# One wait less ahead of the second expert's gathers in a mixture-of-experts kernel

## The chip, the cores and the metric

The kernel runs on one core of one Trainium2 chip. The metric is the device time of one execution in microseconds (us); less is better. The core has five engines, each with its own instruction stream: PE (TensorE, matmuls), DVE (VectorE), ACT (ScalarE), POOL (GpSimd) and SP (SyncE, which here only issues DMAs). They meet at semaphores: an instruction may wait until a semaphore has reached a number, and everything behind it on that engine waits too.

## The reference, cut to what matters

One block of a network on x of 4 x 1024 tokens with 256 features each:

```
x = x + 0.5 * ffn(layernorm(x))
x = x + attention(layernorm(x))        # 16 heads, causal
x = x + 0.5 * ffn(layernorm(x))

# ffn: 8 experts, top 2, capacity C = 1280 tokens for each expert
logits = xf @ Wg ; probs = softmax(logits) ; top_vals, top_idx = top_k(probs, 2)
buf    = tokens put into (expert, place), dropped where place >= C
a, g   = split(buf[e] @ W_in[e])       # 256 -> 2 x 512
out_e  = (gelu(a) * g) @ W_out[e]      # 512 -> 256
y      = sum over the two choices of gate * out_e, back at the token's row
```

Both ffn calls use the same weights, so the kernel runs the same mixture twice, with the attention between them.

## The kernel before, in words

A mixture has two functions. `route` normalizes the tokens, writes them to a table in DRAM (`normalized`, rows of 264 floats: 256 features and the gates), and makes for each expert the list of its 1280 tokens (`token`, 10 tiles of 128 places). It signals `list_ready` = 1 when the first expert's list stands, 2 when those of the seven others do, and 3 when the rows for the way back (`sum_row`) do.

`experts` then goes through the 8 experts, e = 0 to 7, in the same order on each engine:

- POOL brings the expert's rows into SBUF: 10 gathers (indirect DMAs through `gather_slots`, L254), each for 128 rows of 1056 bytes. There are two buffers, `slots[0]` for the even experts and `slots[1]` for the odd ones. Once results are ready it sends them: 10 indirect DMAs (L908) that add 128 result rows each onto the table `sums`. The code has expert e+1's gathers ahead of expert e's sends. The first expert's own gathers are issued by `route` (6) and at the head of `experts` (4).
- PE turns the gathered rows (`transposes`, L1107, in three chunks; each sends one `s_tposed`), multiplies them by W_in (`up`, L1128), and the gated hidden values by W_out (`down`, L1147). float32 values are split into a high and a low part, so each product takes three matmuls. For the first expert the chunks hold 256, 512 and 512 tokens, for the others 512, 512 and 256.
- ACT takes the high part of the turned rows (`s_hi`, L1037), applies the GELU (L1051), takes the high part of the next expert's weights (`w_hi`, L1070) and scales the results (`res`, L1063).
- DVE takes the low parts (`s_lo` L948, `w_lo` L999), multiplies GELU and gate half (`hid`, L968) and splits the product (L971 high, L973 low). PE's `up` has two PSUM buffers: block f may start once DVE's `hid` of block f-2 is done.
- SP loads the next expert's W_in and W_out (1.5 MB, L263 and L265) into the single buffer `raw`, once DVE has done the low parts of the present ones.

The order on each engine is written out by hand. In POOL's loop a gather into `slots` stands behind the condition that the rows that the buffer held have been turned: before expert e+1's gathers POOL waits for `s_tposed` to reach 3 e, which is the count after expert e-1's three chunks. For e = 0, whose gathers fill `slots[1]` for the first time in the mixture, it waits for `list_ready` = 2 and for `s_tposed` = 3, the first expert's three chunks, which are read from `slots[0]`.

Of the kernel before, what the change touches and what calls it, by code (L numbers as in the profile page):

```python
# [250 lines left out]
def gather_slots(pool, held, xn_dram, e, j):  # L251

    at = e * ST + j
    pool.indirect_dma_start(held["slots"][e % 2][:, j * ROW:(j + 1) * ROW], None, xn_dram,  # L254
                            bass.IndirectOffsetOnAxis(ap=held["token"][:, at:at + 1], axis=0)).then_inc(slots_sem(held, e, j), 16)
# [584 lines left out]
def experts(kit, c, r, w_in_dram, w_out_dram, xn_dram, sum_dram, held, out_dram):  # L840
# [4 lines left out]
    with ExitStack() as ctx:  # L845
# [23 lines left out]
        NC, NW = len(CHUNKS), len(W_PARTS)  # L869
# [29 lines left out]
        def gpsimd(pool):  # L899
            last_row = nc.gpsimd.to_reg(TOK + CAP - 1)  # L900

            def send(e, ci):
                c0, n = CHUNKS[ci]
                for j in range(c0 // P, (c0 + n) // P):
                    pool.wait_ge(res_ready, e * ST + j + 1 + RES0)
                    kit.part(pool)
                    at = e * ST + j
                    nc.gpsimd.indirect_dma_start(sum_dram, bass.IndirectOffsetOnAxis(ap=sum_row[:, at:at + 1], axis=0), res[j][:], None,  # L908
                                                 bounds_check=last_row, oob_is_err=True, compute_op=ALU.add).then_inc(added, 16)

            for j in range(EARLY_TILES, ST):
                gather_slots(nc.gpsimd, held, xn_dram, 0, j)
            for e in range(EXP):
                if e + 1 < EXP:
                    if e == 0:
                        pool.wait_ge(list_ready, 2)
                        pool.wait_ge(s_tposed, NC)
                    if e:
                        pool.wait_ge(s_tposed, e * NC)
                    for j in range(ST):  # L920
                        gather_slots(nc.gpsimd, held, xn_dram, e + 1, j)
                if e:
                    pool.wait_ge(added, e * ST * 16)
                else:
                    pool.wait_ge(c["zeroed"], 2 * 16)
                    pool.wait_ge(held["sums_out"], 16)
                    pool.wait_ge(list_ready, 3)
                pool.sem_inc(res_free, 1)
                for ci in range(NC):
                    send(e, ci)  # L930
            pool.wait_ge(added, EXP * ST * 16)
# [164 lines left out]
        def tensor(pe):  # L1096
# [72 lines left out]
            in_turn(nc.tensor, body)  # L1169

        return {"sync": sync, "gpsimd": gpsimd, "vector": vector, "scalar": scalar, "tensor": tensor}

# [1108 lines left out]
```

## Time and profile before

| | |
|---|---|
| three executions, us | 1628.95, 1629.88, 1635.23; median 1629.88 |
| the profiled execution: its own time, its span in the trace, us | 1629.88, 1627.9 |
| PE busy | 1442.2 us (89% of the span) |
| DVE busy | 1022.1 us (63%) |
| ACT busy | 711.3 us (44%) |
| POOL busy | 703.3 us (43%) |
| the 160 gathers on POOL (L254), us | 167.8 busy, mean 1.049 |
| the 160 sends on POOL (L908), us | 271.4 busy, mean 1.696 |
| clock granted to TensorE, mean | 0.941 of full speed |

The first mixture's experts fill about 62 to 430 us of the span and the second's about 1239 to 1610. A gather's or a send's time on POOL is that of making its descriptors; the transfer runs behind it on 16 DMA engines, which all queues share.

### The profile page before, as it was taken

Reading aid. Unit: us, or ns where it says so; the run is one execution under the profiler, and the core shown is the slowest. Engines: PE = TensorE matmul, PEld = TensorE weight load, DVE = VectorE, ACT = ScalarE, POOL = GpSimd, SP = SyncE. Lnnn points to the kernel's source line nnn. Section 1 sums busy time; section 2 is a strip of 40 time slices with the busy share of each in tenths; the row PEclk is TensorE's granted clock in tenths of the full one; section 3 lists DMA queues with packets and bytes.
Section 4 is the critical chain, followed back from the end, with each engine's and each line's share of the span. In section 5 each row is a group of like instructions: output and inputs, shape, how many; then the busy total and the mean of one; then the engine's idle time right before and its main releaser. Section 6 shows DMA issues by size and latency. Waiting matters only on the chain. (4 is left out here: it accounts for less than half of the span.)

```text
span 1627.9 us, 25426 instructions
## 1 busy us (share of the span) xinstructions
PE 1442.2 (89%) x8838; PEld 1085.9 (67%) x8840; DVE 1022.1 (63%) x2599; ACT 711.3 (44%) x1116; POOL 703.3 (43%) x653
## 2 busy tenths in 40 slices
PE   4699999999545799999999999999877999999994
PEld 3588888889544455555555555555556888888884
DVE  7755665555275777777777777886376555665551
ACT  5333333333223055656656565666553333333331
POOL 1375556564423433333333332224303755556533
PEclk9799999999867689999999999999887999999997
DMA  9554444452377936666667568553173544444426
GB/s 313 144 109 96 98 96 65 95 105 33 54 212 210 251 112 165 175 164 163 166 160 183 146 180 246 169 167 92 42 245 81 115 93 96 96 99 64 95 33 136
DMA packets 125559, 218.26 MB, mean 134 GB/s; under 512 B 20232, under 2 KB 86280, under 8 KB 122312
## 3 DMA queue, kind: packets, MB, share of 16 engines
q1 hardware_dynamic: 88824, 165.56, 35.4%
q0 software_dynamic: 30720, 42.62, 16.6%
q10 hardware_dynamic: 5904, 8.66, 1.8%
q8 instruction: 62, 1.02, 0.3%
q14 instruction: 49, 0.40, 0.1%
HBM read 130.56 MB, written 90.14 MB: 136 GB/s over the span
## 5 line engine op out<-in xcount | busy, mean ns | idle before, releaser
L2025 ACT ACTIVATE a_wts<-a_s_psum 128x1024 f32<-128x1024 f32 (+1 forms) x384 | 300.8, 809 | 181.6 <-PE a_s_psum L2142 179.5
L908 POOL DMA_INDIRECT sums<-e_res,e_sum_row x160 | 271.4, 1696 | 245.6 <-ACT e_res L1063 215.7
L1901 DVE CUSTOM_DVE_ANT_0 a_m_psum<-a_m_psum,mask 128x128 f32<-128x128 f32 (+3 forms) x512 | 249.1, 502 | 128.5 <-PE a_m_psum L2117 120.8
L2117 PE MATMUL a_m_psum<-a_kp,a_qp 96*128 96x512 f32 (+2 forms) x768 | 288.6, 410 | 25.2 <-DVE a_parts L1901 9.8
L2117 PEld LDWEIGHTS a_m_psum<-a_kp,a_qp 96*128 96x128 f32 x768 | 148.8, 196 | 144.8 <-DVE a_parts L1901 61.4
L1051 ACT ACTIVATE e_act_a<-e_a_psum 128x512 f32<-128x512 f32 (+1 forms) x192 | 100.4, 527 | 278.2 <-PE e_a_psum L1128 254.0
L1849 POOL TENSOR_SCALAR_AFFINE_SELECT a_wts<-a_wts 128x512 f32<-128x512 f32 x128 | 78.2, 634 | 332.4 <-ACT a_wts L2025 332.4
L968 DVE TENSOR_TENSOR e_hid<-e_act_a,e_g_psum 128x512 f32<-128x512 f32 (+1 forms) x192 | 114.5, 596 | 157.3 <-PE e_g_psum L1128 139.9
L2142 PE MATMUL a_s_psum<-a_qp,a_kp 97*128 97x512 f32 (+2 forms) x768 | 210.0, 356 | 0.4 <-ACT a_wts L2025 0.2
L254 POOL DMA_INDIRECT e_slots<-normalized,e_token x160 | 167.8, 1049 | 92.5 <-issue 46.9
L1147 PE MATMUL e_o_psum<-e_w_hi,e_h_hi 128*128 128x256 f32 x640 | 183.5, 287 | 0.0
L1904 DVE TENSOR_REDUCE a_parts<-a_m_psum 128x1 f32<-128x512 f32 x256 | 176.4, 689 | 9.1 <-PE a_m_psum L2117 6.6
L1147 PE MATMUL e_o_psum<-e_w_hi,e_h_lo 128*128 128x256 f32 x640 | 181.2, 283 | 0.0
L1147 PE MATMUL e_o_psum<-e_w_lo,e_h_hi 128*128 128x256 f32 x640 | 181.2, 283 | 0.0
L2156 PE MATMUL a_o_psum<-a_wts,a_vg 128*17 128x512 f32 (+3 forms) x1536 | 157.2, 497 | 4.2 <-POOL a_wts L1849 2.7
L1128 PE MATMUL e_a_psum<-e_s_hi,e_w_hi 128*128 128x512 f32 (+1 forms) x384 | 141.9, 370 | 18.5 <-DVE e_hid L968 10.0
L2142 PEld LDWEIGHTS a_s_psum<-a_qp,a_kp 97*128 97x128 f32 x768 | 133.5, 191 | 19.0 <-ACT a_wts L2025 4.9
L1063 ACT ACTIVATE e_res<-e_o_psum,e_gate 128x256 f32<-128x256 f32 x160 | 76.0, 475 | 148.7 <-PE e_o_psum L1147 147.7
L1128 PE MATMUL e_a_psum<-e_s_lo,e_w_hi 128*128 128x512 f32 (+1 forms) x384 | 137.3, 358 | 0.0
L1128 PE MATMUL e_a_psum<-e_s_hi,e_w_lo 128*128 128x512 f32 (+1 forms) x384 | 137.1, 357 | 0.0
L1128 PE MATMUL e_g_psum<-e_s_hi,e_w_hi 128*128 128x512 f32 (+1 forms) x384 | 137.0, 357 | 0.0
L1128 PE MATMUL e_g_psum<-e_s_hi,e_w_lo 128*128 128x512 f32 (+1 forms) x384 | 136.8, 356 | 0.0
(270 smaller groups left out, 2560.6 us busy)
## 6 DMA issues: line engine op xcount, KB each, us to landing
packs<-x_res SPq DMA_DIRECT2D x48, 512.0 KB, 5.8
e_w_raw<-in_W_in SPq DMA_DIRECT2D x16, 1024.0 KB, 8.2
a_qp<-packs SPq DMA_DIRECT2D x16, 1024.0 KB, 7.8
a_kp<-packs SPq DMA_DIRECT2D x16, 1024.0 KB, 13.7
e_w_raw<-in_W_out SPq DMA_DIRECT2D x16, 512.0 KB, 8.3
normalized<-r_xn SPq DMA_DIRECT2D x16, 512.0 KB, 4.4
sums<-x_res SPq DMA_DIRECT2D x2, 4096.0 KB, 16.5
x_res<-sums SPq DMA_DIRECT2D x8, 1024.0 KB, 11.3
```

The source lines that it names most:

```text
L254: pool.indirect_dma_start(held["slots"][e % 2][:, j * ROW:(j + 1) * ROW], None, xn_dram, bass.IndirectOffsetOnAxis(ap=held["token"][:, at: ...
L908: nc.gpsimd.indirect_dma_start(sum_dram, bass.IndirectOffsetOnAxis(ap=sum_row[:, at:at + 1], axis=0), res[j][:], None, bounds_check=last_r ...
L968: nc.vector.tensor_tensor(hid[q][:, 0:n], act_a[q][:, 0:n], g_ps[q][:, 0:n], ALU.mult).then_inc(hid_done, 1)
L1051: nc.scalar.activation(act_a[q][:, 0:n], a_ps[q][:, 0:n], ACT.Gelu).then_inc(gelu_done, 1)
L1128: last = nc.tensor.matmul(bank[q][:, 0:n], w_in_at(w, k, half + f), s[:, k, c0:c0 + n], start=(z == 0), stop=(z == len(terms) - 1))
L1147: last = nc.tensor.matmul(o_ps[(u * ST + c0 // P + j) % 2][:, 0:D], s[:, k, j * P:(j + 1) * P], w_out_at(w, k), start=(z == 0), stop=(z == ...
L1901: nc.vector.tensor_tensor_reduce(products, products, c["mask"][:, QC - width:], 1.0, MASKED, ALU.add, ALU.max, top).then_inc(max_read, 1)
L1904: nc.vector.reduce_max(top, products, AX.X).then_inc(max_read, 1)
L2025: nc.scalar.activation(wts[(u * NS + s) % 2][:, j, 0:w], s_ps[q % 2][:, 0:w], ACT.Exp).then_inc(weighed, 1)
L2117: nc.tensor.matmul(m_ps[bank((n, h, z))][:, 0:stream], qp[n % NB][0:PACK, h, qt * P:(qt + 1) * P], kp[n % NB][0:PACK, h, part * QC:part * ...
L2142: last = nc.tensor.matmul(s_ps[q % 2][:, col - lead:col + w], kp[u][:, j, kt * P:(kt + 1) * P], qp[u][:, j, at - lead:at + w], start=True, ...
L2156: last = nc.tensor.matmul(o_ps[j * HP:j * HP + HV, q0:q0 + w], vg[u][:, kt, j, :], wts[(u * NS + s) % 2][:, j, col:col + w], start=(kt == ...
```

## The change

In `experts`, in POOL's stream, the wait for `s_tposed` = 3 ahead of the second expert's gathers is taken out. It stood once in each mixture, so the program loses two waits. The wait for `list_ready` = 2 stays, and so do the waits of all later experts.

```diff
                 if e + 1 < EXP:
                     if e == 0:
                         pool.wait_ge(list_ready, 2)
-                        pool.wait_ge(s_tposed, NC)
                     if e:
                         pool.wait_ge(s_tposed, e * NC)
                     for j in range(ST):
```

On POOL, at the head of the first mixture's experts, the rows are the following (a piece of the difference; `e_slots` are the buffers, `normalized` the table of rows, `x9` nine equal instructions, `experts_s_tposed` the semaphore of the wait):

```order
 L254 DMA e_slots<-normalized,e_token 128x264 [waits route_list_ready,route_gates_out,route_rows_out]
 L254 DMA e_slots<-normalized,e_token 128x264 x9
-L254 DMA e_slots<-normalized,e_token 128x264 [waits experts_s_tposed,route_list_ready]
+L254 DMA e_slots<-normalized,e_token 128x264 [waits route_list_ready]
 L254 DMA e_slots<-normalized,e_token 128x264 x9
 L908 DMA sums<-e_res,e_sum_row 5376x256 [waits route_list_ready,const_zeroed,route_sums_out,experts_res_ready]
```

No instruction has another place. The first of the second expert's ten gathers has one condition less; the ten sends of the first expert stand behind them as before. The other engines' streams are the same but for line numbers.

## Rows read from the trace of the kernel before

**Rows 1.** Timeline of POOL, first mixture: start us, us, instruction, [idle before <-releaser]

```profile
68.56 0.95 POOL L254 DMA_INDIRECT e_slots<-normalized,e_token  x1 [0.30 <-issue]
82.23 1.46 POOL L254 DMA_INDIRECT e_slots<-normalized,e_token  x1 [12.73 <-PE e_tp_psum L1107]
...
95.55 0.94 POOL L254 DMA_INDIRECT e_slots<-normalized,e_token  x1 [0.30 <-issue]
96.79 1.63 POOL L908 DMA_INDIRECT sums<-e_res,e_sum_row  x1 [0.30 <-issue]
...
104.32 1.56 POOL L908 DMA_INDIRECT sums<-e_res,e_sum_row  x1 [4.01 <-ACT e_res L1063]
...
117.34 1.55 POOL L908 DMA_INDIRECT sums<-e_res,e_sum_row  x1 [0.30 <-issue]
```

**Rows 2.** Timeline of POOL, second mixture

```profile
1241.42 1.59 POOL L254 DMA_INDIRECT e_slots<-normalized,e_token  x1 [0.30 <-issue]
1257.98 1.47 POOL L254 DMA_INDIRECT e_slots<-normalized,e_token  x1 [14.97 <-PE e_tp_psum L1107]
```

**Rows 3.** Waits of PE, 67 to 118 us: engine, line, releaser: total us, times, longest

```profile
PE e_a_psum L1128 <- DVE e_hid L968: 0.2, 1, 0.2
```

**Rows 4.** Timeline of PE, first mixture, and a row of the second

```profile
74.86 0.47 PE L1128 MATMUL e_a_psum<-e_s_hi,e_w_hi 128*128 128x512 f32 x1 [0.20 <-DVE e_hid L968]
...
81.23 0.48 PE L1128 MATMUL e_a_psum<-e_s_hi,e_w_hi 128*128 128x512 f32 x1
...
84.05 0.39 PE L1128 MATMUL e_a_psum<-e_s_hi,e_w_hi 128*128 128x512 f32 x1
...
100.55 1.03 PE L1107 MATMUL e_tp_psum<-ident,e_slots 128*128 128x128 f32 x8
...
1256.98 0.47 PE L1128 MATMUL e_a_psum<-e_s_hi,e_w_hi 128*128 128x512 f32 x1
```

**Rows 5.** Stretches: A:B, us, PE, PEld, DVE, ACT, POOL busy (count), PEclk, DMA share, GB/s

```profile
60.00:64.00 4.00, 2.10 (x29) 1.71 (x26) 1.08 (x3) 1.14 (x1) 3.06 (x4) 1.00 0.40 109
...
70.00:72.00 2.00, 2.00 (x20) 2.00 (x19) 1.00 (x3) 0.56 (x2) 0.00 (x0) 1.00 1.09 415
72.00:74.00 2.00, 2.00 (x19) 2.00 (x18) 1.93 (x5) 1.15 (x3) 0.00 (x0) 1.00 0.97 311
74.00:76.00 2.00, 1.80 (x11) 1.44 (x10) 1.90 (x6) 1.25 (x2) 0.00 (x0) 1.00 0.17 55
```

**Rows 6.** Timeline of ACT, first and then second mixture

```profile
73.98 0.38 ACT L1051 ACTIVATE e_act_a<-e_a_psum 128x256 f32<-128x256 f32 x1 [0.85 <-PE e_a_psum L1128]
75.12 1.05 ACT L1070 CAST e_w_hi<-e_w_raw 128x1024 fp32r<-128x1024 f32 x1 [0.75 <-DMA e_w_raw<-in_W_out]
76.53 0.60 ACT L1051 ACTIVATE e_act_a<-e_a_psum 128x512 f32<-128x512 f32 x1 [0.36 <-PE e_a_psum L1128]
...
88.48 0.47 ACT L1063 ACTIVATE e_res<-e_o_psum,e_gate 128x256 f32<-128x256 f32 x1 [1.35 <-PE e_o_psum L1147]
...
1250.31 1.04 ACT L1070 CAST e_w_hi<-e_w_raw 128x1024 fp32r<-128x1024 f32 x1
1252.29 0.60 ACT L1051 ACTIVATE e_act_a<-e_a_psum 128x512 f32<-128x512 f32 x1 [0.94 <-PE e_a_psum L1128]
```

**Rows 7.** A stretch of the second mixture, same columns

```profile
1248.00:1250.00 2.00, 2.00 (x19) 2.00 (x18) 1.07 (x1) 1.18 (x2) 0.00 (x0) 1.00 0.43 150
```

**Rows 8.** Timeline of DVE, first and then second mixture

```profile
78.08 0.69 DVE L968 TENSOR_TENSOR e_hid<-e_act_a,e_g_psum 128x512 f32<-128x512 f32 x1 [1.46 <-PE e_g_psum L1128]
...
81.00 0.68 DVE L968 TENSOR_TENSOR e_hid<-e_act_a,e_g_psum 128x512 f32<-128x512 f32 x1
...
1253.83 0.69 DVE L968 TENSOR_TENSOR e_hid<-e_act_a,e_g_psum 128x512 f32<-128x512 f32 x1 [1.44 <-PE e_g_psum L1128]
```

**Rows 9.** One of DVE's groups, 82 to 98 us: busy us, mean ns | idle

```profile
L971 DVE CAST e_h_hi<-e_hid 128x512 fp32r<-128x512 f32 x5 | 2.4, 474 | 0.2
```

**Rows 10.** The same group, 98 to 119 us

```profile
L971 DVE CAST e_h_hi<-e_hid 128x512 fp32r<-128x512 f32 x3 | 1.3, 426 | 0.1
```

## The prediction

> **What bounds the kernel now.** I read the timeline of POOL first, since the change stands there. After its last gather for the first expert (start 68.56 us) POOL sits idle for 12.73 us until PE's third chunk of transposes, then issues the second expert's ten gathers from 82.23 to 96.49 (95.55 + 0.94), and goes straight on to the sends [rows 1]. The second mixture has the same picture, with 14.97 us of idle time [rows 2]. The change opens these two gaps. Idle time of an engine is worth something only if another one waits for it, so the next view is that of PE's waits: from 67 to 118 us, which covers the gap, the gathers and the sends, PE waits once, 0.2 us, for DVE [rows 3]. It never waits for a gather. PE turns the second expert's rows at 100.55 [rows 4], 4.1 us after POOL is done with the gathers, and runs into that instruction with no idle time. So in this stretch the kernel goes at PE's pace, and neither POOL nor the gathered rows set it. What earlier gathers could still do is disturb somebody, so the last views are the DMA share by stretch, ACT's and DVE's timelines and DVE's durations beside gathers.
>
> **The start of the gathers.** The one wait left is for the lists of the seven other experts. POOL's queue has the first expert's gathers ahead of it, the last of them ending at 68.56 + 0.95 = 69.5, and the lists must stand by then, since PE is busy without a gap with the first expert's products from 70 on [rows 5], and its part in the lists comes ahead of them in its stream. With the 0.30 us between two gathers the second expert's begin at about 69.8 in place of 82.2, 12.4 us earlier, and end at about 84.1. In the second mixture they begin at 1241.42 + 1.59 + 0.30 = 1243.3 in place of 1258.0, 14.7 us earlier. Worth to PE: 0, because the rows were there in time already.
>
> **The sends behind them.** The first result is ready at 88.48 + 0.47 = 88.95 [rows 6], but its send starts at 96.79, behind the gathers [rows 1]. It will start at about 89.0, 7.8 us earlier, and the second soon after. The third waits for ACT again, 4.01 us, and starts at 104.32, and from there the sends run one behind the other to the last at 117.34. ACT's results come from PE, so the third and the last stay where they are. The lead of the first two is lost again within the expert; the gathers for the third expert, which follow the last send, don't move. Worth 0.
>
> **The weights of the second expert.** This is the one transfer that the moved gathers run into. SP loads 1.5 MB for ACT, and ACT waits for it already: it is free at 73.98 + 0.38 = 74.36 and starts the high part at 75.12, released by that DMA [rows 6]. The DMA engines are full from 70 to 74 (shares 1.09 and 0.97) and at 0.17 from 74 to 76, so the load ends at about 74.3 [rows 5]. Gathers alone, at POOL's pace, take 0.40 of the engines and move 109 GB/s (60 to 64 us, same rows). The first moved gather's descriptors are out at about 70.8. From then 3.5 us of full engines are left of the load; with 0.6 of the engines that is 3.5 / 0.6 = 5.8 us, a delay of 2.3 us. If both get halves it is 7.0 us, a delay of 3.5.
>
> How much of a delay does PE not see? The high part would end at 76.17, the GELU behind it starts at 76.53 because PE is not ready before: 0.36 us. That GELU ends at 77.13, and DVE's product starts at 78.08, held by PE [rows 8]: 0.95 us. The product ends at 78.77 and frees the PSUM buffer that PE takes at 81.23: 2.46 us. Together 3.8. The next product, 81.00 to 81.68, has 2.37 us to PE's 84.05, with DVE busy in between: 0.36 + 0.95 + 2.37 = 3.7. So delays of 2.3 and 3.5 both cost nothing, the latter barely; the cover is gone from 3.7 on, and then each microsecond counts.
>
> In the second mixture ACT does not wait for the load: it starts at 1250.31 [rows 6], and the share of 0.43 from 1248 to 1250 says that the load ends at about 1248.9 [rows 7]. From 1244.3, when the moved gathers begin to transfer, 4.6 us are left; over 0.6 that is 7.7 us, to 1252.0, 1.7 us after ACT's start (with halves 9.2 us, 3.2 after). The slack is 0.94 up to the GELU at 1252.29, 0.94 up to the product at 1253.83 [rows 8], and from its end, 1254.5, to PE at 1256.98 [rows 4] 2.46: together 4.3. Again 0.
>
> **DVE beside POOL's gathers.** While ten gathers ran (82 to 98 us) DVE's copy of 512 columns took 474 ns as a mean of five [rows 9]; from 98 to 119, beside sends, it took 426 [rows 10]. That is 0.05 us each, 0.24 for the five. This disturbance moves to 70 to 84 us. From 70.9 to 76.6 DVE goes without a pause and PE waits for it (the 0.2 us at 74.86 [rows 4]), so there a share of it reaches PE; further on DVE's products have 2.4 us to PE's need. About half of the gathers fall into the tight part: 0.12 us a mixture, 0.2 for both. The bounds are +0.5 (all ten, both mixtures) and -0.4 (PE's wait of 0.2 gone in both; I have no mechanism for more, since PE has no other idle time to give back). I take +0.2, near the measured copies.
>
> The Trainium skill has a rule that speaks against this change: in "SBUF — State Buffer", section "SBUF: two separate sides", the port pair of DVE and GpSimd is an exclusive lock, and the loser is blocked for the whole instruction. By it a copy that meets a gather would wait up to the gather's full time. The trace bears out at most a small part of that, with 48 ns more on the mean copy; it is the second rival below.
>
> **Sum.** The profiled execution took 1629.88 us (span 1627.9, 2.0 around it), which is also the median of the three runs. Gathers 0, sends 0, weights 0, DVE +0.2: 1630.1 us. Changes below 0.5% (8.1 us) are what a measurement of this kernel can't tell from none; one run of three was itself 5.3 above the median.
>
> **Rivals.**
>
> *The weights come too late (slower).* Place: ACT's high part of the second expert's weights, both mixtures. It decides from a delay of 3.7 us in the first and 4.3 in the second. If the load got nothing until all ten gathers were issued, it would end at 84.1 + 3.5 = 87.6, a delay of 13.3, and PE would lose 9.6; in the second mixture, with 14.3 us for ten gathers as in the first, 1243.3 + 14.3 + 4.6 = 1262.2 against 1250.3, 11.9, and a loss of 7.6. Together 17.2, that is 1647.1 at the far end. I price it at half: 1638.5. For it: ACT already waits 0.75 us for that DMA and the engines are full just then. Against: the gathers come at POOL's pace and leave 0.6 of the engines. 4%.
>
> *DVE is held by the gathers (slower).* Seven copies of DVE (four of 256 columns, three of 512) fall between 70 and 82 us (PE's blocks there, one copy each; an estimate from its pace). Were each held for a whole gather of 0.95, DVE would be 6.7 us late, less 2.4 of slack: 4.3 a mixture, 8.6 in all, 1638.5. Against it are rows 9. 3%.
>
> *The first two sends count (faster).* If the first expert's end hung on its sends, 7.8 us would be gained in each mixture: 1614.3. For it: the first result waits 7.8 us for POOL. Against: POOL waits for ACT before the third send, and PE waits for nothing. 2%.
>
> *Nothing moves.* The gathers start no earlier because another condition holds POOL (the lists, or room for descriptors in its queue): 1629.9. The 12.73 us are put down to PE's transposes, which speaks against. 3%.
>
> **How the numbers follow.** 88% for the forecast, 1630.1. Its own spread is the scatter of the runs rather than the terms: 1628.0 to 1634.5 holds it 8 or 9 times in 10 and leaves out the two slower rivals and the faster one, together 9%. Slower by over 0.5%: the two slower rivals at their price and above, with what an unlucky set of runs adds, 5%. Faster by over 0.5%: 3%. Within: 92%.
>
> **What the next profile would show.** Right: POOL's idle time before the second expert's gathers gone, their starts near 69.8 and 1243.3; the first send near 89, the third still near 104.3 with its wait for ACT; PE's transposes of the second expert still near 100.5; ACT's first high part of the second expert later by 1 to 3 us, with a longer wait for the DMA, and PE's blocks at 81.2 and 84.0 unmoved. Wrong: PE waiting several microseconds for DVE or ACT between 78 and 90 us (the weights), DVE's copies near 1 us (the lock), or PE's transposes of the second expert more than a microsecond away from 100.5.

## The result, and the profile after

| | before | after |
|---|---|---|
| executions, us | 1628.95 to 1635.23, median 1630.58 (4) | 1649.62 to 1659.21, median 1657.14 (4) |
| ratio, 95% interval | | 1.0156 (1.0134 to 1.018) |
| profiled execution, its span, us | 1629.88, 1627.9 | 1641.82, 1640.0 |
| granted TensorE clock, mean | 0.941 | 0.934 |

Beside the profiled one and these four, ten more executions of the changed kernel are on record, 1654.98 to 1664.46 us. The ratios here and in the experiments are the record's estimates, each with its interval, and not quotients of the two medians (that would be 1.0163 here).

The changed kernel is 1.56% slower. The prediction was 1630.1 us, 1628.0 to 1634.5: no change. POOL's timeline of the changed kernel, first mixture (start, us, instruction, [idle before <-releaser]):

```profile
68.35 0.94 POOL L254 DMA_INDIRECT e_slots<-normalized,e_token  x1 [0.30 <-issue]
69.60 0.95 POOL L254 DMA_INDIRECT e_slots<-normalized,e_token  x1 [0.30 <-issue]
...
80.89 0.95 POOL L254 DMA_INDIRECT e_slots<-normalized,e_token  x1 [0.30 <-issue]
103.96 1.73 POOL L908 DMA_INDIRECT sums<-e_res,e_sum_row  x1 [22.12 <-ACT e_res L1062]
...
118.46 1.57 POOL L908 DMA_INDIRECT sums<-e_res,e_sum_row  x1 [10.33 <-ACT e_res L1062]
...
131.48 1.55 POOL L908 DMA_INDIRECT sums<-e_res,e_sum_row  x1 [0.30 <-issue]
```

The gathers did what was foreseen: the second expert's begin at 69.60 where 12.73 us of idle time stood [rows 1], and all twenty stand in one row, most of them 1.25 us apart. But the sends come later than before, not earlier: the first at 103.96 instead of 96.79, the last at 131.48 instead of 117.34. POOL now waits 22.12 us for ACT. So look at the engines ahead of ACT. PE's waits from 67 to 118 us, and the two rows they are made of:

```profile
PE e_a_psum L1127 <- DVE e_hid L967: 11.3, 2, 6.4
```

```profile
79.50 0.58 PE L1127 MATMUL e_a_psum<-e_s_hi,e_w_hi 128*128 128x256 f32 x1 [6.42 <-DVE e_hid L967]
...
87.33 0.77 PE L1127 MATMUL e_a_psum<-e_s_hi,e_w_hi 128*128 128x512 f32 x1 [4.91 <-DVE e_hid L967]
```

Before there was 0.2 us of such waiting [rows 3]. PE's transposes of the second expert come at 114.69 instead of 100.55 [rows 4], so 14.1 us are lost by then. The clock fell too. Stretches of the changed kernel (PE, PEld, DVE, ACT, POOL busy, PEclk, DMA share, GB/s):

```profile
74.00:76.00 2.00, 0.00 (x0) 0.00 (x0) 0.00 (x0) 0.38 (x1) 1.39 (x3) 1.00 0.89 325
76.00:78.00 2.00, 0.00 (x0) 0.00 (x0) 0.00 (x0) 0.00 (x0) 1.70 (x2) 0.81 0.48 120
78.00:80.00 2.00, 0.50 (x2) 0.50 (x3) 0.91 (x3) 0.00 (x0) 1.39 (x3) 0.50 0.31 87
82.00:86.00 4.00, 0.43 (x3) 0.13 (x1) 0.36 (x1) 1.41 (x3) 0.00 (x0) 0.50 0.23 49
```

From 76 to 78 us PE, DVE and ACT all do nothing, and only POOL runs. After PE has stood still the granted clock is 0.50 (the 1.2 GHz level), and the first matmuls behind the two waits are slow: 0.58 us with 256 columns, where the one at 71.41 took 0.36, and 0.77 us with 512 columns in place of the 0.47 of before [rows 4]. Where three engines stand idle together, the question is who has finished and was not heard. Here are PE's rows and ACT's, side by side:

```profile
70.62 1.04 PE L1106 MATMUL e_tp_psum<-ident,e_slots 128*128 128x128 f32 x8
...
72.80 0.28 PE L1127 MATMUL e_g_psum<-e_s_hi,e_w_lo 128*128 128x256 f32 x1
```

```profile
67.63 0.38 ACT L1050 ACTIVATE e_act_a<-e_a_psum 128x256 f32<-128x256 f32 x1 [0.96 <-PE e_a_psum L1127]
74.05 0.38 ACT L1050 ACTIVATE e_act_a<-e_a_psum 128x256 f32<-128x256 f32 x1 [6.04 <-remote]
84.59 1.01 ACT L1036 CAST e_s_hi<-e_tp_psum 128x1024 fp32r<-128x1024 f32 x1 [10.16 <-remote]
85.50 0.67 ACT L1050 ACTIVATE e_act_a<-e_a_psum 128x256 f32<-128x256 f32 x2
86.04 1.06 ACT L1069 CAST e_w_hi<-e_w_raw 128x1024 fp32r<-128x1024 f32 x1
```

PE's transposes end at 70.62 + 1.04 = 71.66. ACT's copy of them, which needs only their signal and an idle ACT, starts at 84.59: 12.9 us later. The block that ends at 72.80 + 0.28 = 73.08 is heard at about the same time, since ACT then runs two GELUs without a pause. DVE is in the same position; its product waits 7.15 us for a block that PE had ended at 70.78:

```profile
70.66 0.42 DVE L967 TENSOR_TENSOR e_hid<-e_act_a,e_g_psum 128x256 f32<-128x256 f32 x1 [2.31 <-remote]
...
79.02 0.42 DVE L967 TENSOR_TENSOR e_hid<-e_act_a,e_g_psum 128x256 f32<-128x256 f32 x1 [7.15 <-remote]
```

The sum of the profiled execution, from the view of ACT's copies `e_s_hi` (24 a mixture; the two times are the first and the last start), before and then after:

```profile
L1037 ACT CAST e_s_hi<-e_tp_psum x24: 585/1014/1016, 65.0 to 398.9; 128x1024 fp32r<-128x1024 f32 x16, 128x512 fp32r<-128x512 f32 x8
L1037 ACT CAST e_s_hi<-e_tp_psum x24: 585/1014/1018, 1239.7 to 1574.2; 128x1024 fp32r<-128x1024 f32 x16, 128x512 fp32r<-128x512 f32 x8
```

```profile
L1036 ACT CAST e_s_hi<-e_tp_psum x24: 585/1014/1017, 64.8 to 409.1; 128x1024 fp32r<-128x1024 f32 x16, 128x512 fp32r<-128x512 f32 x8
L1036 ACT CAST e_s_hi<-e_tp_psum x24: 586/1014/1017, 1249.1 to 1586.3; 128x1024 fp32r<-128x1024 f32 x16, 128x512 fp32r<-128x512 f32 x8
```

333.9 becomes 344.3 and 334.5 becomes 337.2: +10.4 and +2.7, against +12.1 of the span. The median of the other executions lies 15 above the profiled one; a later profile of the same kernel (e11 below, span 1650.0) has 344.1 and 343.8, so there both mixtures lose about 10.

### The profile page after: what moved, and what is told of

Its sections match the earlier page's. It is cut to its first block and busy times, and to the rows that moved or that the text cites. A ratio compares the mean times of both kernels' runs of the same rounds, so it can differ in the third digit from the quotient of the medians.

```text
span 1640.0 us, 25426 instructions
## 1 busy us (share of the span) xinstructions
PE 1448.2 (88%) x8840; PEld 1088.4 (66%) x8840; DVE 1023.1 (62%) x2599; ACT 711.9 (43%) x1116; POOL 696.8 (42%) x653
## 5 line engine op out<-in xcount | busy, mean ns | idle before, releaser
L908 POOL DMA_INDIRECT sums<-e_res,e_sum_row x160 | 268.0, 1675 | 288.5 <-ACT e_res L1062 260.1
L1127 PE MATMUL e_g_psum<-e_s_lo,e_w_hi 128*128 128x512 f32 (+1 forms) x384 | 137.7, 359 | 0.0
## 6 DMA issues: line engine op xcount, KB each, us to landing
x_res<-sums SPq DMA_DIRECT2D x8, 1024.0 KB, 11.6
```

Of the source, the lines that this page charges most:

```text
L1127: last = nc.tensor.matmul(bank[q][:, 0:n], w_in_at(w, k, half + f), s[:, k, c0:c0 + n], start=(z == 0), stop=(z == len(terms) - 1))
```

## The experiments

All came with the kernel before on the same chip. They ran in six sessions on five chips, which turned out to matter: 1 to 4 on chip 12, 5 to 8 on chip 7, 9 and 10 on chip 1, 11 to 13 on chip 15, 14 and 15 on chip 8, 16 and 17 on chip 12 again. The theory after the result: PE's signals are late behind a long run of indirect gathers (A). The first rivals were the transfer of the weights that the gathers now meet (B), and any ten DMAs of POOL at that place (C).

**e1_small_w.** The second expert's weights load cut down:

```diff
+                if e == 1:
+                    for a, d in ((0, w_in[... 0:16]), (NIN, w_out[... 0:16])):
+                        nc.sync.dma_start(held["raw"][:, a:a + 16], d).then_inc(w_loaded, 16)
+                    continue
                 load_weights(nc.sync, held, w_in_dram, w_out_dram, e, w_loaded)
```

> The kernel without the wait, and of the second expert's weights SP loads only 16 columns of each matrix in each mixture (the rest of the buffer keeps the first expert's weights). Theory A, the moved gathers hold back TensorE's completion signals by themselves: the time stays near 1655 us (the loss over before, about 25 us, is there to at least two thirds) and in the profile ACT's turning copy of the first expert's second chunk starts 5 us or more after PE's transposes. Theory B, the collision of gathers and weights' load: the loss goes, time within 5 us of 1630.

Measured 1655.64 us against 1628.34, ratio 1.0159 (1.0124 to 1.0195). All of the loss is there without the load, and so are the late signals: ACT's copy starts 13.1 us after its transposes end (72.77), and it and the GELU ahead of it wait 8.15 and 7.43 us for nothing that the profile shows.

```profile
77.31 0.38 ACT L1055 ACTIVATE e_act_a<-e_a_psum 128x256 f32<-128x256 f32 x1 [7.43 <-remote]
85.85 1.01 ACT L1041 CAST e_s_hi<-e_tp_psum 128x1024 fp32r<-128x1024 f32 x1 [8.15 <-remote]
```

B falls.

**e2_plain_dma.** The ten early gathers as plain copies of 128 table rows each, on the same queue (the second expert gets other rows):

```diff
                     for j in range(ST):
+                        if e == 0:
+                            nc.gpsimd.dma_start(slots[1][:, j * ROW:(j + 1) * ROW], xn_dram[j * P:(j + 1) * P, :]).then_inc(...)
+                            continue
                         gather_slots(nc.gpsimd, held, xn_dram, e + 1, j)
```

> The kernel without the wait, and the second expert's ten early gathers are ten direct copies of 128 rows each from the same table, same bytes, destination, queue (POOL's) and place (the second expert so gets other tokens). Theory A in its form that any transfer of POOL's queue in this place does it: about 1650 us and late signals again. Theory A in its form that the indirect addressing does it (one descriptor for each row, made by GpSimd from the list): within 5 us of 1630. Theory B (contention with the weights' load): like the gathers, about 1650, since the bytes are the same.

Measured 1630.54, ratio 1.0001 (0.9978 to 1.0023). POOL issues the ten in 5.43 us. The same bytes at the same place, sooner still, cost nothing, though ACT does wait for the weights:

```profile
70.47 5.43 POOL L921 DMA_DIRECT2D e_slots<-normalized  x10
```

```profile
72.86 1.01 ACT L1039 CAST e_s_hi<-e_tp_psum 128x1024 fp32r<-128x1024 f32 x1 [0.65 <-PE e_tp_psum L1109]
...
77.98 1.05 ACT L1072 CAST e_w_hi<-e_w_raw 128x1024 fp32r<-128x1024 f32 x1 [2.58 <-DMA e_w_raw<-in_W_out]
```

C falls: ten DMAs of this queue with the same bytes are not enough. Here the weights do come later: from SP's issue of the load (68.43) to ACT's start it is 9.55 us, where before it was 7.66 (67.46 to 75.12). These 1.9 us of delay stay inside the slack of 3.7 that the prediction had worked out: PE waits 0.3 us for DVE.

**e3_spaced.** POOL fills a scrap tile (1.18 us) ahead of each of the ten:

```diff
                     for j in range(ST):
+                        if e == 0:
+                            link(nc.gpsimd.memset(pad[:], 0.0))
                         gather_slots(nc.gpsimd, held, xn_dram, e + 1, j)
```

> The kernel without the wait, and POOL clears a scratch tile of 128x1280 (about 1.2 us) ahead of each of the second expert's ten gathers, so that they go out at about half the rate, 70 to 95 us. Theory A by backlog (twenty gathers in a row are more than the path to the semaphores takes): the late signals shrink, time 1630 to 1643. Theory A by presence (a gather in flight beside the first expert's first products): as long or longer, 1650 or more. Theory B: half the bytes beside the weights' load, so half the loss, about 1643.

Measured 1640.35, ratio 1.0066 (1.0036 to 1.0095), inside the range of A by backlog. But what is left of the loss is no late signal. The copy of the transposes starts at 73.31, 0.03 us after they end (71.78 + 1.50). What is slow is DVE's copy of 256 columns: it takes up to 1.88 us here, against 0.29 in the changed kernel, and the one below ends at 75.98, 0.14 us after POOL's fill.

```profile
73.31 1.02 ACT L1040 CAST e_s_hi<-e_tp_psum 128x1024 fp32r<-128x1024 f32 x1 [1.98 <-PE e_tp_psum L1110]
```

```profile
74.19 1.79 DVE L974 CAST e_h_hi<-e_hid 128x256 fp32r<-128x256 f32 x1
74.66 1.18 POOL L923 MEMSET e_pad<- 128x1280 f32 x1
```

That makes DVE late with its products: PE waits 1.9 us for one of them in the first mixture and 2.0 in the second, and its granted clock is at 0.50 from 80 to 82 us. So with a gather every 2.4 to 2.6 us the signals come in time, and these rows put the loss that remains on the fills that I put in as pauses.

**e4_from_second_chunk.** All ten early, but only after two of the three groups of transposes:

```diff
                     if e == 0:
                         pool.wait_ge(list_ready, 2)
+                        pool.wait_ge(s_tposed, 2)
```

> The wait stands again but asks for two of the three chunks of transposes, so that the second expert's gathers begin when the first expert's second chunk is turned (about 72 us in the trace of before, in place of 69.8 or 82.2). Theory A by place (the first expert's first products and second chunk of transposes are what suffers): most of the loss goes, under 1640. Theory A by presence: the signals of the products behind suffer in place of it, 1640 to 1655. Theory B: the gathers still meet the weights' load from 72 to 75, about half the loss, 1640.

Measured 1631.44, ratio 1.0012 (0.9995 to 1.0029), as A by place expected; A by presence (1640 to 1655) falls. One pause of 3.11 us between the two tens is enough:

```profile
69.67 0.95 POOL L254 DMA_INDIRECT e_slots<-normalized,e_token  x1 [0.31 <-issue]
73.72 0.99 POOL L254 DMA_INDIRECT e_slots<-normalized,e_token  x1 [3.11 <-PE e_tp_psum L1107]
```

```profile
73.00 1.02 ACT L1037 CAST e_s_hi<-e_tp_psum 128x1024 fp32r<-128x1024 f32 x1 [0.68 <-PE e_tp_psum L1107]
...
85.30 1.02 ACT L1037 CAST e_s_hi<-e_tp_psum 128x1024 fp32r<-128x1024 f32 x1 [3.74 <-remote]
```

The copy that was 12.9 us late comes at once. The ten then make signals late again, the copy at 85.30 by 2.7 us and the GELU behind it by 4.2, where 512-column blocks cover it: PE doesn't wait for DVE in this stretch.

**e5_narrow.** Gathers of 24 elements in place of 264:

```diff
+                        if e == 0:
+                            nc.gpsimd.indirect_dma_start(slots[1][:, j * ROW:j * ROW + 24], None,
+                                xn_dram.rearrange("r (a b) -> (r a) b", b=24), IndirectOffsetOnAxis(token ...)).then_inc(...)
+                            continue
```

> The changed kernel, but the ten early gathers of the second expert fetch 24 elements of each row instead of 264 (1/11 of the bytes, the same 1280 rows and ten instructions; the second expert computes on zeros beside them, and POOL fills the buffer with zeros once before the routing ends). Theory A (what matters is that POOL issues indirect gathers one after another, 128 rows each, not what they carry): the signals of TensorE are again up to 8 to 12 us late between 70 and 85 us, PE waits over 10 us in all in the first chunks of both mixtures, time 1.012 to 1.018 of before (1648 to 1658 us). Rival D (the gathered bytes fill the DMA engines or the memory that the signals share): 1/11 of the bytes leaves under 1 us of lateness, time 0.998 to 1.003 (1625 to 1634 us).

Measured 1612.72 against 1607.82, ratio 1.0022 (1.0004 to 1.004); PE has no wait for DVE in the stretch. The kernel also has POOL fill the buffer with zeros once in each mixture, which may be the 0.2%. A had expected 1.012 to 1.018, so read alone the run would speak for D. The next three runs show that it can't be read so.

**e6_extra_ten.** The kernel before, with ten more gathers behind those of expert 3:

```diff
                         gather_slots(nc.gpsimd, held, xn_dram, e + 1, j)
+                    if e == 3:
+                        for j in range(ST):
+                            nc.gpsimd.indirect_dma_start(pad[:, j * ROW:(j + 1) * ROW], None, xn_dram, IndirectOffsetOnAxis(token ...)).then_inc(pad_in, 16)
```

> The kernel before, with ten more gathers right behind the usual ten of expert 3 in both mixtures, into a buffer that nobody reads: 20 without a pause, but in a 512-column stretch of the steady experts, far from the mixture's start. Theory A (lateness grows with the number of gathers issued without a pause, wherever they stand): instead of 2.7 to 3.5 us as behind the usual ten, TensorE's signals come 6 to 12 us late near the end of the 20; blocks of 2.7 us, two in flight, cover about 3 us of that, so PE waits 4 to 9 us more in that expert, and its pitch grows from 45.6 to 50 to 56 us; time of the kernel 1.005 to 1.012 of before. Rival E (the place counts: only the mixture's start, with the second weights load and short chunks, is vulnerable): lateness stays near 3 us, no wait, the kernel's time 1.000 to 1.002.

Measured 1608.33, ratio 0.9998 (0.998 to 1.0016), no lateness. This too is outside what A had expected.

**e7_first_mixture.** `s_tposed` = 3 is waited for in the second mixture alone:

```diff
                         pool.wait_ge(list_ready, 2)
+                        if r:
+                            pool.wait_ge(s_tposed, NC)
```

> The change in the first mixture alone; the second keeps the wait for the third transpose group. Theory A: each mixture loses for itself, so half to 60% of the loss stays, the first mixture as in the changed kernel (first send near 104 us, last of the first expert near 131), the second as before; time 1.006 to 1.010 of before (1638 to 1645 us). Rival F (the loss is in one mixture, or is something of the whole program such as the code's or buffers' places): all of it stays (1.014 to 1.018) or none (0.998 to 1.002).

Measured 1607.45, ratio 1.0006 (0.9982 to 1.003). In its first mixture twenty gathers stand in one row exactly as in the changed kernel, and nothing is late. A had not expected that; of F, the case "none" fits, which says nothing of why. What differs is the kernel before itself: it takes 1607.8 us here and took 1628 to 1631 until now.

**e8_interleaved.** An attempt at a better kernel: four gathers of each batch where ten stood, the others one by one behind the sends:

```diff
-                    for j in range(ST):
+                    for j in range(4):
                         gather_slots(nc.gpsimd, held, xn_dram, e + 1, j)
...
                         nc.gpsimd.indirect_dma_start(sum_dram, ...).then_inc(added, 16)
+                    if e + 1 < EXP and j + 4 < ST:
+                        gather_slots(nc.gpsimd, held, xn_dram, e + 1, j + 4)
```

> The kernel before, wait kept, but each expert's batch of ten gathers is cut: four are issued where the ten stood, and one more behind each of that expert's first six sends. The mean rate of gathers is the same; the longest run without a pause is four. Theory A: the lateness of 2.7 to 3.5 us at the end of each batch falls under 1.2 us, and the 0.3 to 0.4 us of PE wait that each steady expert shows there goes; pitch of an expert 45.6 us or 0.3 to 0.6 us less, over 13 experts and two mixtures 0 to 9 us; time 0.994 to 1.000 of before. Rival G (lateness comes from the rows still queued, not from a run, or the later gathers of tiles 4 to 9 delay the next expert's transposes): lateness stays, and time 1.000 to 1.010.

Measured 1626.82 against 1607.82, ratio 1.011 (1.0082 to 1.0137), slower than A (to 1.000) and G (to 1.010) had it, and not by lateness: the gathers now wait behind sends, which wait for results, and come too late for PE, as this row of its timeline shows.

```profile
108.58 1.97 PE L1110 MATMUL e_tp_psum<-ident,e_slots 128*128 128x128 f32 x8 [4.97 <-DMA e_slots<-normalized,e_token]
```

**e9_change_again.** The changed kernel itself, unedited.

> The changed kernel itself, beside the kernel before. In the runs of the previous set the kernel before took 1607.8 us instead of 1628 to 1631, its steady experts 44.6 us instead of 45.6, and 20 gathers in a row (the change in the first mixture) left no signal of TensorE late; so either (A2) late signals behind POOL's gathers are something that one chip shows and another doesn't, or (F) the change in one mixture is harmless and only in both, or in the second, does it lose. If this run falls on a chip where before takes about 1608: A2 expects 0.998 to 1.003, no consumer of TensorE more than 1.5 us late between 60 and 100 us; F expects 1.012 to 1.018. If it falls on one where before takes about 1629: both expect 1.012 to 1.018, and the run beside it decides.

Measured 1608.42 against 1609.46, ratio 0.9994 (0.9979 to 1.0008). **On this chip the change costs nothing.** ACT's rows:

```profile
68.60 1.01 ACT L1036 CAST e_s_hi<-e_tp_psum 128x1024 fp32r<-128x1024 f32 x1 [1.21 <-PE e_tp_psum L1106]
...
73.52 1.05 ACT L1069 CAST e_w_hi<-e_w_raw 128x1024 fp32r<-128x1024 f32 x1 [2.38 <-DMA e_w_raw<-in_W_out]
```

The copy starts as soon as the transposes end, PE has no wait from 67 to 118 us, and POOL's gathers stand in one row, as before. A2 holds and F falls: the same program is slower on one chip and not on another.

**e10_extra_again.** The kernel of e6, on the same chip as e9.

> Once more the kernel before with ten more gathers behind the usual ten of expert 3 in both mixtures. On a chip where before takes about 1629 us, A2 expects signals 6 to 12 us late near the end of the 20, PE waiting 4 to 9 us more in that expert, 1.004 to 1.012; the rival that the place counts (E) expects lateness as behind the other tens, 1.000 to 1.002. On a chip where before takes about 1608 us both expect what the run before showed, 1.000, and it tells nothing new but that it repeats.

Measured 1610.93, ratio 1.0011 (0.9994 to 1.0028); as expected for such a chip.

**e11_change_third.** The changed kernel once more.

> The changed kernel once more, in another session. Theory A2 (what decides is whether the chip shows late TensorE signals behind a run of POOL's gathers; where it does, the kernel before takes about 1629 us, its steady experts 45.0 to 45.6 us, and where it doesn't 1608 and 44.6): with before near 1629, 1.012 to 1.018; with before near 1608, 0.998 to 1.002. Rival H (the session or the program's load decides, not the chip: lateness comes and goes without a link to before's own time): any mix of the two, e.g. before near 1608 and the change 1.5% slower.

Measured 1644.78 against 1623.1, ratio 1.0119 (1.0065 to 1.0173). The lateness is back: ACT's copy of the transposes starts 12.9 us after they end, and PE waits in both mixtures.

```profile
84.84 1.01 ACT L1036 CAST e_s_hi<-e_tp_psum 128x1024 fp32r<-128x1024 f32 x1 [10.86 <-remote]
```

```profile
PE e_a_psum L1127 <- DVE e_hid L967: 10.1, 1, 10.1
```

(The second is PE's wait from 1235 to 1300 us.) The ratio is at the lower edge of what A2 expected (1.012). The same program text, byte for byte, loses 1.2 to 1.6% on one kind of chip and nothing on the other, and the median time of the kernel before says which it is: rival H finds no support.

**e12_first_again.** The kernel of e7.

> The change in the first mixture alone, once more. With before near 1629 us, A2 expects each mixture to lose for itself: 1.006 to 1.010, PE waiting over 10 us in the first mixture's first chunks and not in the second's. With before near 1608 us it repeats 1.000 and tells nothing new.

Measured 1637.99, ratio 1.0088 (1.0052 to 1.0124). In the first mixture PE waits 11.6 us for DVE, in the second it never waits for DVE. Each mixture loses for itself.

**e13_extra_third.** The kernel of e6.

> Ten more gathers behind the usual ten of expert 3, once more. With before near 1629 us, A2 expects TensorE's signals 6 to 12 us late near the end of the 20 instead of 2.7 to 3.5 behind ten, 4 to 9 us more of waiting in that expert, 1.004 to 1.012; the rival that only the mixture's start is vulnerable (E) expects 1.000 to 1.002. With before near 1608 us both expect 1.000.

Measured 1641.33, ratio 1.0117 (1.0073 to 1.0162). Here twenty gathers stand in the middle of the steady experts, far from the mixture's start, and ACT's GELU is held the same way, the second one until 12.0 us after the end of its block (225.57):

```profile
227.66 0.60 ACT L1057 ACTIVATE e_act_a<-e_a_psum 128x512 f32<-128x512 f32 x1 [6.90 <-issue]
237.53 0.60 ACT L1057 ACTIVATE e_act_a<-e_a_psum 128x512 f32<-128x512 f32 x1 [9.27 <-remote]
```

The first mixture's copies run from 65.7 to 407.8, 342.1 us against 333.9. The run's length decides, not the place: E falls.

**e14_paced and e16_paced_again.** The kernel before, each steady batch of ten tied to ScalarE's GELUs:

```diff
                     for j in range(ST):
+                        if e:
+                            pool.wait_ge(gelu_done, e * NC * KF + 1 + j * 7 // ST)
                         gather_slots(nc.gpsimd, held, xn_dram, e + 1, j)
```

> The kernel before, but the ten gathers of each expert from the third on wait one by one or in pairs for ScalarE's gelus (the wait grows by 7 blocks over the ten), so that they spread over some 20 us of the first two blocks of matmuls instead of 12.5 and no run is longer than two. A2, on a chip that shows lateness (before 1623 to 1631 us): lateness behind each batch falls from 2 to 3.5 us to under 1.2, the steady experts' pitch from 45.0 to 45.6 to about 44.6, time 0.992 to 0.998 of before. On a chip that shows none (before near 1608): 0.999 to 1.002. Rival J (the chip's longer pitch is not from late signals): 0.999 to 1.003 on both.

Measured on chip 8 (before: 1608.53): 1608.23, ratio 1.0001 (0.9986 to 1.0016).

> The paced gathers once more. With before at 1623 to 1631 us (a chip that shows lateness) A2 expects lateness under 1.2 us behind each batch, steady pitch about 44.6 us, time 0.992 to 0.998 of before; rival J 0.999 to 1.003. With before near 1608 us both expect 1.000, as in the run before.

Measured on chip 12: 1617.96 (12 runs) against 1623.27 (18), ratio 0.9989 (0.9965 to 1.0013). The lateness behind the batches is gone; ACT's GELUs come every 2.72 us, where in the kernel before one was held for 5.46 and then two ran together. Of the two fences the first is the kernel before, the second the paced one.

```profile
172.60 0.59 ACT L1051 ACTIVATE e_act_a<-e_a_psum 128x512 f32<-128x512 f32 x1
178.65 1.08 ACT L1051 ACTIVATE e_act_a<-e_a_psum 128x512 f32<-128x512 f32 x2 [5.46 <-PE e_a_psum L1128]
```

```profile
171.12 0.60 ACT L1053 ACTIVATE e_act_a<-e_a_psum 128x512 f32<-128x512 f32 x1 [2.10 <-PE e_a_psum L1130]
173.84 0.60 ACT L1053 ACTIVATE e_act_a<-e_a_psum 128x512 f32<-128x512 f32 x1 [2.12 <-PE e_a_psum L1130]
```

In the profiled execution the mixtures take 328.4 and 327.5 us against 333.9 and 334.5 before. But these executions on chip 12 scatter widely (the kernel before from 1613.86 to 1628.78). The quotient of the medians is 0.9967, inside A2's range of 0.992 to 0.998; the estimate, 0.9989, lies between it and J's 0.999, and its interval holds both and 1. So a gain is not shown, and A2 and J are not told apart.

**e15_five_early and e17_five_again.** Five gathers early, five behind the old wait:

```diff
                     for j in range(ST):
+                        if e == 0 and j == ST // 2:
+                            pool.wait_ge(s_tposed, NC)
                         gather_slots(nc.gpsimd, held, xn_dram, e + 1, j)
```

> Half of the change: five of the second expert's ten gathers go ahead of the wait for the third transpose group, five stay behind it, so that 15 stand in a row instead of 20. A2, on a chip that shows lateness: signals 4 to 8 us late between 68 and 80 us instead of up to 13.9, PE waits 2 to 8 us per mixture instead of about 15, time 1.002 to 1.009 of before. On a chip that shows none: 0.998 to 1.002.

Measured on chip 8: 1608.75, ratio 0.9999 (0.9987 to 1.0012).

> Five of the ten gathers early, once more. With before at 1623 to 1631 us A2 expects signals 4 to 8 us late, 2 to 8 us of waiting per mixture, 1.002 to 1.009 of before; with before near 1608 us 1.000 again.

Measured on chip 12: 1636.63, ratio 1.0081 (1.0047 to 1.0115).

```profile
75.31 0.38 ACT L1052 ACTIVATE e_act_a<-e_a_psum 128x256 f32<-128x256 f32 x1 [6.73 <-remote]
77.57 1.01 ACT L1038 CAST e_s_hi<-e_tp_psum 128x1024 fp32r<-128x1024 f32 x1 [1.88 <-remote]
```

The copy starts 6.1 us after its transposes (71.51), and PE waits 5.1 us for DVE. So on the chips that show it, the lateness at the end of a run is 2 to 4 us behind ten gathers, 6 to 7 behind fifteen, 12 to 13 behind twenty.

## Why the prediction was wrong

- **What bounds the kernel: right.** PE's pace does. POOL's idle time and the gathers' early data were worth nothing: on chip 1 the change is at 0.9994.
- **Start of the gathers: right.** 69.8 was forecast, 69.60 came, with 0.30 us to the one before. In the second mixture too they follow without a gap, though that mixture itself stands some 13 us later by then.
- **The sends: the mechanism right, the rows wrong.** With nothing late (e9) the first send starts at 86.29, directly after its result, and POOL waits 10.34 us for ACT before the third, which is worth nothing. On the chip of the result the results themselves come late, and the first send starts 7.2 us after that of before.
- **The weights: the 0 came out, the delay didn't.** A delay of 2.3 to 3.5 us inside a slack of 3.7 was forecast. In e9 ACT waits 2.38 us for the load, but the kernels of e6 and e14, whose first mixture is that of the kernel before up to there, wait 2.64 and 2.42, also on chips without lateness; from SP's issue to ACT's start it is 7.87 us in e9, 8.13 in e6 and 7.91 in e14. So the moved gathers didn't delay the load, and that this term was right is luck. That a delay is covered, e2 shows for 1.9 us. The rival fell as well: without the load (e1) the loss remains.

```profile
73.39 1.05 ACT L1076 CAST e_w_hi<-e_w_raw 128x1024 fp32r<-128x1024 f32 x1 [2.64 <-DMA e_w_raw<-in_W_out]
```

- **DVE beside the gathers: a mean read as a cost of each.** The 474 ns of [rows 9] are four copies at 0.43 us and one at 0.65, so most copies beside gathers took what they take elsewhere. In e9 DVE's copy of 512 columns takes 451 ns as a mean of seven between 68 and 98 us and 427 between 84 and 116, and whatever this is worth doesn't show in the time. By the exclusive lock of the Trainium skill ("SBUF — State Buffer", "SBUF: two separate sides"), which that page states for DVE's instructions in a two-port mode among others, a copy that meets a gather would wait up to the gather's 0.95 us. The trace of the changed kernel doesn't show that: a copy of 256 columns that lies inside the gather of 70.85 to 71.80 takes 0.29 us. Beside POOL's fills (e3) such copies are held, up to 1.88 us.

```profile
71.11 0.29 DVE L970 CAST e_h_hi<-e_hid 128x256 fp32r<-128x256 f32 x1
```

- **The step that failed** is a term that the sum didn't have: "what earlier gathers could still do is disturb somebody, so the last views are the DMA share, ACT's and DVE's timelines and DVE's durations". It looked for disturbance in durations and transfers. The disturbance was in the signals between engines, in which no instruction gets longer: ACT's copy starts 12.9 us after its transposes, and PE waits 11.3 us for DVE in the first mixture alone. It is worth 0 on one kind of chip and 12 to 27 us on the other, by the profiled run and the median.
- **"PE waiting several microseconds for DVE or ACT between 78 and 90 us (the weights)"** was the sign named for the weights rival. The sign came, with another cause: in the changed kernel ACT starts the weights' high part at 86.04 straight behind a GELU, without a wait. A wait of PE for DVE names the last link of a chain; the chain has to be walked back to its source.

It could have been seen. The kernel before, on the chip of the result, has the mechanism at small size. This is ACT's copy of the very first chunk:

```profile
64.99 0.58 ACT L1037 CAST e_s_hi<-e_tp_psum 128x512 fp32r<-128x512 f32 x1 [3.85 <-remote]
```

PE's transposes had ended at 62.87, 2.1 us before the copy started, and at 178.65 ACT's two GELUs in a row (the fence above) come 3.4 us after the end of the first one's block, 175.26. Each time a run of gathers was under way. The change takes away the pause between two such tens, at a place where the first expert's blocks of 256 columns leave PE little to live on. With that the sum could have had a price instead of a 0, if lateness grows with the run, as it does in the later runs, and PE's two buffers cover a block or two of it.

**What stays open.** Whether it is a property of those chips, or of what else ran beside the kernel there, can't be told from these runs; chip 12 showed it in both of its sessions, chip 15 in its one, chips 1, 7 and 8 never. Nor do they show what carries the signals and the gathers' work in common. The ends of matmuls are modelled in the profile, so a signal sent late and one that travels long look alike. That ten plain copies of the same bytes at the same place don't do it is shown (e2); whether the bytes of the gathers matter is not, since e5 fell on a chip without lateness.

One rival stands untested: the recording itself. The kernel before (as in the result), the changed kernel and every run on chips 12 and 15 have 15,455 to 16,065 records of semaphore updates in the trace; every run on chips 1, 7 and 8 has 17,506 to 17,836. Of the signal that PE sends 48 times behind its transposes the former have 35 to 40 records and the latter 49 or 50 (two of them not behind transposes). So exactly the runs with late signals also lose records of signals. Every execution on record comes with a span and a granted clock, and none is known to have run unrecorded, so the lateness, and with it the loss of time, could belong to the recording on those chips as well as to the kernel.

## What to carry to other kernels

Before idle time of a DMA-issuing engine is closed, ask what the pause gave to the others, and keep runs of indirect DMAs short beside engines that hand over small blocks: one pause of 3 us between two tens was enough here. A pause made of work costs on its own: the fills of e3 held DVE. Where several engines stand idle together, compare the end of each producer with the start of its idle consumer; a gap of microseconds that the profile puts down to "remote" or "issue" is a late signal, and it already stands in the profile of before if you look. A difference of 1 to 2% should be measured on more than one chip, with the kernel before beside it each time.

## What the runs showed of the hardware

- Completion signals of TensorE arrive up to 13 us after the modelled end of the matmuls while GpSimd issues twenty indirect gathers of 128 rows one every 1.25 us; they come in order, and the last five within 0.3 us of each other (84.57 to 84.87) as the last gather lands (84.77). Signals from ACT to DVE and from DVE to PE were not late in the same stretch (copy ended 65.37, DVE started 65.40; product ended 79.44, PE started 79.50). Behind ten plain copies on the same queue (e2), and with a gather every 2.4 to 2.6 us (e3), the recorded signals come within 0.02 us of the modelled ends once the first ten gathers are through.
- This differs from chip to chip: two chips of five show it (and that of the result, whose number isn't on record). There the median of the kernel before is 1623 to 1631 us, on the others 1607.8 to 1609.5. The first mixture's copies span 333.9 us there and 326.4 in e9 (63.2 to 389.6), the second's 334.5 and 326.3; that is 15.7 of the 22.3 us between the two profiled spans.
- While PE stood idle from 73.08 to 79.50 its granted clock went from 1.00 (74 to 76 us) over 0.81 to 0.50 (78 to 80, the 1.2 GHz level), and it was still 0.50 from 82 to 86. So a late signal is paid twice, by the wait and by slower matmuls behind it.
- A copy on DVE (256 columns) takes 0.29 us inside a gather's instruction of GpSimd and 1.79 to 1.88 where a gather and a fill of 1.18 us follow one another; it then ends 0.14 to 0.15 us after the fill (e3).
